# Second attention of a fused two-layer block: the scalings of a batch move into the route of the batch ahead, ranks move behind the values, the output bias becomes one product, and the powers on GpSimd change place

## The reference

```
x = x + 0.5 * _L0_ffn_ref(_layernorm(x), ...)
x = x + _L0_attn_ref(_layernorm(x), ...)
x = x + 0.5 * _L0_ffn_ref(_layernorm(x), ...)
x = x + 0.5 * _L1_ffn_ref(_layernorm(x), ...)
x = x + _L1_attn_ref(_layernorm(x), ...)          # the change is here
x = x + 0.5 * _L1_ffn_ref(_layernorm(x), ...)     # its route overlaps the line above

def _L1_attn_ref(x, Wq, bq, Wk, bk, Wv, bv, Wo, bo):
    q, k, v = x @ Wq + bq, x @ Wk + bk, x @ Wv + bv
    # 7 windows of 128 rows, each 64 rows on from the last
    scores = einsum('bwqd,bwkd->bwqk', q[win], k[win]) / sqrt(8)
    out_w = einsum('bwqk,bwkd->bwqd', softmax(scores), v[win])
    out = (sum of the windows over each row) / counts
    return out @ Wo + bo

def _L1_ffn_ref(x, router_w, router_bias, ...):
    scores = softmax(x @ router_w.T + router_bias)          # 32 experts
    topk_scores, topk_idx = top_k(scores, 4)
    ...                                                     # the 4 experts' outputs, weighted, and 4 shared experts
```

## Time and profile before

| | us |
|---|---|
| median of 3 runs | 938.57 (936.98 to 939.16) |
| the profiled execution | 937.39 |
| its span | 936.2 |
| PE busy | 765.0 (82%) |
| DVE busy | 545.2 (58%) |
| ACT busy | 427.6 (46%) |
| POOL busy | 495.7 (53%) |

### The profile page before, as it was taken

The page is one execution under the profiler, slowest core; times in us unless marked ns, Lnnn a source line. Parts: engine busy times, 40 slices in busy tenths (PEclk is TensorE's granted clock), DMA queues, the critical chain, the costliest instruction groups (busy, mean ns, idle before and its releaser), DMA issues.

```text
span 936.2 us, 18891 instructions
## 1 busy us (share of the span) xinstructions
PE 765.0 (82%) x6432; PEld 622.5 (66%) x6432; DVE 545.2 (58%) x1655; ACT 427.6 (46%) x1099; POOL 495.7 (53%) x488
## 2 busy tenths in 40 slices
PE   6889978999999998798997999727888997999600
PEld 5778746589877876677775888614566775888500
DVE  6875576668577668977773444305855563444305
ACT  3667545656055536465422666501433322666500
POOL 5655630026291026376672677775177751677773
PEclk9999989999799989999999999958988999999955
DMA  9999999800140050011114444215011112444216
GB/s 227 218 217 212 224 220 220 179 4 4 48 135 1 2 158 1 1 47 41 45 56 111 124 122 126 72 53 185 1 50 50 50 43 74 120 124 123 75 53 230
DMA packets 125757, 94.67 MB, mean 101 GB/s; under 512 B 10624, under 2 KB 116480, under 8 KB 125664
## 3 DMA queue, kind: packets, MB, share of 16 engines
q1 hardware_dynamic: 113472, 71.19, 32.9%
q0 software_dynamic: 10176, 21.65, 6.7%
q10 hardware_dynamic: 2016, 0.63, 0.3%
HBM read 34.05 MB, written 59.38 MB: 100 GB/s over the span
## 4 chain that ended last, share of the span: by engine, by line
PE 47%; DVE 22%; POOL 14%; issue 9%; ACT 5%; DMA 2%; SPq 0%; POOLq 0%; DVEq 0%; ACTq 0%
POOL expert_rows L677 9%; PE banks L1638 5%; PE banks L1110 3%; POOL sorted_rows L445 3%; PE banks L1685 3%; PE banks L1667 3%; PE banks L624 3%; PE banks L783 3%; PE banks L172 3%; PE banks L396 3%; PE banks L397 2%; PE banks L398 2%; DVE h L744 2%; PE banks L793 2%; ACT sg L691 2%
## 5 line engine op out<-in xcount | busy, mean ns | idle before, releaser
L677 POOL DMA_INDIRECT expert_rows<-y,goal x190 | 181.9, 957 | 96.5 <-issue 53.7
L445 POOL DMA_INDIRECT sorted_rows<-rows_x,row_of x128 | 128.3, 1003 | 76.5 <-DVE row_of L500 40.2
L990 ACT ACTIVATE ys<-banks,wtab 128x128 f32<-128x128 f32 x256 | 73.0, 369 | 66.7 <-PE banks L1110 56.7
L744 DVE TENSOR_TENSOR h<-sg,banks 128x512 f32<-128x512 f32 x48 | 33.0, 687 | 97.3 <-ACT sg L691 97.3
L396 PE MATMUL banks<-x_high,w_high 128*128 128x512 f32 x192 | 85.3, 444 | 0.6 <-POOL w_low L880 0.6
L1110 PE MATMUL banks<-w,hT 128*128 128x128 f32 x512 | 72.9, 287 | 14.0 <-DVE hT L1031 13.9
L1110 PEld LDWEIGHTS banks<-w,hT 128*128 128x128 f32 x512 | 66.4, 197 | 23.3 <-DVE hT L1031 20.8
L915 POOL TENSOR_TENSOR x<-ys,x 128x512 f32<-128x512 f32 x44 | 56.3, 1280 | 45.2 <-ACT ys L990 44.7
L398 PE MATMUL banks<-x_high,w_low 128*128 128x512 f32 x192 | 76.8, 400 | 0.0
L397 PE MATMUL banks<-x_low,w_high 128*128 128x512 f32 x192 | 76.6, 399 | 0.0
L172 PE MATMUL banks<-wqkv,ident 128*128 128x384 f32 x122 | 53.0, 592 | 26.2 <-DMA expert_rows<-y,goal 19.4
(11 more groups left out here) (300 smaller groups left out, 1884.4 us busy)
## 6 DMA issues: line engine op xcount, KB each, us to landing
sorted_rows<-zeros SPq DMA_DIRECT2D x32, 1120.0 KB, 17.1
tile<-sorted_rows SPq DMA_DIRECT2D x192, 70.0 KB
routed_low<-in_ffn_w SPq DMA_DIRECT2D x8, 512.0 KB, 3.8
w<-in_ffn_w SPq DMA_DIRECT2D x20, 192.0 KB, 3.9
expert_rows<-y,goal POOLq DMA_INDIRECT x190, 2.2
routed_down<-in_ffn_w SPq DMA_DIRECT2D x8, 256.0 KB, 5.2
sorted_rows<-rows_x,row_of POOLq DMA_INDIRECT x128
xnT<-expert_rows SPq DMA_DIRECT2D x2, 1024.0 KB, 5.7
```

Source lines behind the costliest of these rows:

```text
L445: POOL.indirect_dma_start(sorted_rows, bass.IndirectOffsetOnAxis(self.row_of[:, g, i:i + 1], 0), rows_x[:, 4 * g + i % 4, :], None).then_i ...
L677: POOL.indirect_dma_start(expert_rows, bass.IndirectOffsetOnAxis(goal[:, 4 * q + i:4 * q + i + 1], 0), y[q % 6][:, i * P:(i + 1) * P], Non ...
L990: last = SCL.mul(ys[s % 2][:, j * P:(j + 1) * P], bank[4 + s % 2][:, j * P:(j + 1) * P], wtab[:, t, e:e + 1])
```

## The change

- The loop over batches on DVE: `scale(b, 0)` and `scale(b, 1)` stand behind the pieces "scores" and "top" of the route of group b-1, no longer behind all of its pieces.
- `vector_low(b - 1)` stands behind `residual(b)` and the piece "variance".
- PE: `tensor_rank(b - 1)` stands behind `values(b, 1)`, no longer ahead of `turned(b, 0)`; of the two `keep_busy(3, ...)` around it, one with 2 products is left.
- `output`: one 128x512 product of ones with the bias row, broadcast over the four blocks, comes ahead of the wait for `oT`; the four 128x128 products with `Wo` add to it.
- POOL: the next group's power comes behind the 3rd transfer of group 0, the 1st of group 1 and the 1st of group 2, no longer behind the 8th.

```diff
-                for b, transfers in enumerate((8, 8, 8, 0)):
+                for b, transfers in enumerate((3, 1, 1, 0)):
                     srt.pool_dispatch(b, transfers)
...
                         maximum(b, 0)
                         maximum(b, 1)
-                        for piece in Sorted.VECTOR[2:]:
+                        for piece in ("scores", "top"):
                             routed_piece(b - 1, piece)
                         scale(b, 0)
                         scale(b, 1)
-                        srt.vector_low(b - 1)
+                        for piece in ("hot", "counted", "weights", "rows"):
+                            routed_piece(b - 1, piece)
                     residual(b)
                     routed_piece(b, "variance")
+                    if b:
+                        srt.vector_low(b - 1)
...
                 def output(b):
+                    PE.wait_ge(*(norm.ready(b + 1) if b + 1 < B else srt.norm.ready(b - 1)))
+                    PE.matmul(bank[6][:, :], ones[:, :], bo_row[:, :].unsqueeze(1).broadcast_to([P, TB, D]), start=True, stop=False,
+                              skip_group_check=True)
                     PE.wait_ge(*oT_ready(b + 1))
-                    PE.wait_ge(*(norm.ready(b + 1) if b + 1 < B else srt.norm.ready(b - 1)))
                     for j in range(TB):
-                        po = bank[6][:, j * P:(j + 1) * P]
-                        PE.matmul(po, oT[b % 2][:, j * P:(j + 1) * P], wo1[:, :], start=True, stop=False)
-                        last = PE.matmul(po, ones[:, :], bo_row[:, :], start=False, stop=True)
+                        last = PE.matmul(bank[6][:, j * P:(j + 1) * P], oT[b % 2][:, j * P:(j + 1) * P], wo1[:, :], start=False,
+                                         stop=j == TB - 1, skip_group_check=True)
...
-                        keep_busy(3, bank[5 - b % 2])
-                        srt.tensor_rank(b - 1)
-                        keep_busy(3, bank[5 - b % 2])
+                        keep_busy(2, bank[5 - b % 2])
                     turned(b, 0)
                     turned(b, 1)
                     values(b, 0)
                     values(b, 1)
+                    if b:
+                        srt.tensor_rank(b - 1)
                     if b < LAST:
                         project_q(b + 1)
                     output(b)
```

## The result

The changed kernel took 926.1 us (median of 4 runs, 923.33 to 929.95) beside 938.87 us for the kernel before (4 runs, 936.98 to 940.64): ratio 0.9877, 95% interval 0.9836 to 0.9918. Forecast were 924.9 us and a range of 923.0 to 932.0. The four executions stand in two pairs: 923.33 and 923.53 us at a mean granted clock of 0.925, 928.67 and 929.95 at 0.919 and 0.917. The profile is of the first pair: 923.53 us (span 922.3) against 937.39 (936.2, 0.928), 13.9 us less, where the sum gave 13.7. The second pair left no profile.

The account below looks back on a forecast made before the run. Two paths bounded the routed experts' start, PE's loop with shared steps and POOL's 64 transfers; with PE's loop shorter, POOL bounds. The tiles' turn moves from 783.21 to 769.5, 13.7 us sooner: 938.57 becomes 924.9 us, range 923.0 to 932.0.

Parts of the forecast that it names:

- the sum: POOL's transfers and powers, data, issue and landing added up: tiles' turn at 769.5 against 783.21, 13.7 us sooner.
- Scalings within the route: DVE's scalings start behind "top", so PE's `turned` comes 5.12 us sooner in batch 1; group 0's rows wait 1.49 us longer.
- Ranks behind the values: On PE, the 0.91 us rank moves behind the values without a wait, putting 0.91 us ahead of q and output.
- Bias as one product: One 512-column product of 0.86 us on PE, ahead of oT: no PE time saved, 0.5 us gained in batch 0.
- Fillers: Four of six PE fillers per batch go; they stood in waits for DVE and cost nothing if the clock holds.
- `vector_low`: Its 0.68 us go into DVE's 2.17 us wait for the power; delays batch 3's first shared `hT` by 0.6 us.
- Powers: On POOL, group 1's power comes at 683.8 without POOL waiting; group 1's transposes at 686.2, 5.3 us sooner.
- POOL is the bound: From group 1's transposes POOL's transfers and powers set the pace; transposes of group 2 at 704.9, group 3 from 726.2.
- The landing: First tiles' data arrive 3.9 us after SP's issue, between 3.2 and 6.05, so the turn comes at 769.5.
- (a): PE's clock stays low from group 1's transposes to batch 2's output, POOL waits 6.2 us: 931.1 us; chance 0.14.
- (b): PE's clock low throughout, from group 0's transposes to the shared steps: 5.4 us slower, 944.0 us; chance 0.03.
- (c): Powers or rows late through an unseen wait; PE's loop 2 us shorter a batch, not 5: 934.5 us; chance 0.09.

Follow-up runs that it names:

- e4: Changed kernel with the ranks again ahead of the transposes of the scaled weights (`turned`): 939.86 us, ratio 0.9964 to the kernel before.
- c2: Changed kernel measured again without any edit, on a third chip: 932.38 us, ratio 0.9864 to the kernel before.
- e6: Changed kernel without the 2 filler products ahead of `turned`: 936.75 us, ratio 0.9915 to the kernel before.
- f1: Changed kernel with the powers again behind 8 transfers of each group: 952.03 us, ratio 1.0076 to the kernel before.
- f2: Kernel before with only the powers moved, behind transfers 3, 1 and 1: 940.46 us, ratio 0.9960 to the kernel before.
- c1: Changed kernel again without any edit, in a session with all times much longer: 1085.43 us, ratio 0.9936 to the kernel before.
- c3: Changed kernel again without any edit, in another session with all times much longer: 1072.98 us, ratio 0.9969 to the kernel before.
- e3: Changed kernel with 2 more filler products ahead of each routed group's transposes, in a slow session: 1088.20 us, ratio 0.9970 to the kernel before.
- e5: Changed kernel with the output bias again as four products behind oT's wait, in a slow session: 1080.20 us, ratio 1.0022 to the kernel before.
- g1: Changed kernel, 3 filler products ahead of `turned`, 2 more ahead of transposes in batches 2 and 3, slow session: 1075.23 us, ratio 0.9981 to the kernel before.

## Why the prediction was right

| step | predicted | measured |
|---|---|---|
| `turned`, batch 1 | 673.84 | 673.81 |
| output's end, batch 1 | 680.3 | 680.28 |
| POOL's first transfer | 679.8 | 679.80 |
| power, group 1 | 683.8 | 683.37 |
| transposes, groups 1, 2, 3 | 686.2, 704.9, 726.2 to 726.8 | 685.79, 704.55, 726.05 |
| powers, groups 2, 3 | 702.5, 723.8 | 702.14, 723.64 |
| POOL's end, data | 764.0, 765.4 | 764.07, 765.41 |
| issue, turn of tiles | 765.6, 769.5 | 765.63, 769.34 |

**Scalings within the route** held to 0.03 us, with the wait of 1.3 us. **Ranks behind the values** took 0.81 us, not 0.91, and nobody waited for them but DVE in batch 3 (0.26 us). `e4` shows that the place matters more than its expectation had it. No run moves the scalings alone; their 5.1 us are read from the rows. **Bias as one product**: 0.86 us as taken, 0.5 gained in batch 0. **Fillers** cost nothing in the profiled execution; that part of the step was too sure, since with the same program the clock fell in `c2` and took 1.5 us. **`vector_low`** stood in a wait. **Powers**: the first came 0.4 us early, because POOL's first transfer took 1.03 us and not the 1.44 of the earlier trace rows, and the powers of groups 2 and 3 were 0.4 and 0.2 early with it; by the end that was given back, since two transfers took 1.16 and 1.15 us and one 1.01 instead of 0.96. That POOL's end came out to 0.1 us is in this part luck: two sizes were off and cancelled. The variance of group 2 was called just in time, at 701.9 to 702.7; it was there at 700.65, 1.5 us ahead of its power. From transposes to `turned` the sum took 6.0 us "as in batch 1" and 0.6 for a low clock, but its own batch 1 gives 5.49 (668.85 to 674.34), and it was 5.48 again. The power did not wait, so the time is the same. **POOL is the bound**: no gap over 0.31 us. The filler ended at 768.49 and PE then stood 0.85 us for tiles, so the data path decides. The landing took 3.71 us from the issue, where 3.9 was taken between 3.2 and 6.05.

The median of 926.1 is 1.2 us above the forecast, because two of the four executions took some 5 us more than the other two. The sum has no term for that. It had said that 0.2% could be told from no change; the interval came out at 0.4% to either side.

Of the rivals, (a) had the clock low from group 1's transposes to output. They did bring a low clock (`keep_busy` at 688.58 took 2.77 us for its 2 products, 1.46 in batch 1), but `turned` at 691.27 ran at full speed again (1.22 us), 0.91 over the batch. The slow filler only used up what had been 1.31 us of wait in batch 1, so the fall cost nothing. The Trainium skill (TensorE: Matmul & The Clock Gate, Part 4: PE-mode transpose) says that transposes do not count as busy for the clock as products do. By that rule rival (a)'s 931.1 should have come; the trace gave the forecast's time, and the falls in `c2` and `e6` came at transposes with 1.31 and 2.60 us of idle ahead of them, so no run here tells the rule from the idle. Rival (b), low clock throughout, is what `e4` has in part (0.91, 0.85, 0.80 by batch): still 0.4% faster than before. Rival (c) didn't come either in the changed kernel; `e4` is nearest to it, with `turned` meeting a wait, and lost 7.5 us beside 934.5 less 924.9 = 9.6.

What the prediction didn't say is how little its two main steps are worth apart: the powers alone gained 4.7 us by the medians, the order alone lost 7.1. It added their effects on one timeline, which was right for both together.

## What to carry to other kernels

Where a queue does two jobs, look for a ring: the producer's work waits for something that stands in the queue behind the consumer's items. Add up the pieces of the ring from the trace; if they make the period exactly, a faster producer alone is worth nothing, and a change of order that delays the items makes it slower. Then lay the changed timeline out to the queue's end and ask which engine has no gap left. Ask it again for each part of the change alone: here the turn waited for POOL's path in the changed kernel, `c2` and `e6`, and for PE's in the kernel before, `f1`, `f2` and `e4`.

## What the runs showed of the hardware

- PE's granted clock fell or held for the same instructions with the same idle of 1.31 us: 13.0 or 11.47 us to the rows, in 4 and 3 profiles.
- Of the powers on POOL for the routed groups, all 14 that began within 0.2 us of the start of DVE's `vector_low` (L507) took 1.41 us (`c1`, `c3`, `e3` to `e6`, `g1`); the others took 1.04 or 1.05, also behind waits of 5.32 and 2.85 us in `f2`, where `vector_low` is done by then. In the changed kernel it ends 0.08 us before the first power.
- The first indirect transfer after a wait took 1.44 us in the kernel before, where `scale` (L1863) ran on DVE as it began (678.62 to 679.31), and 1.03 in the changed one, where DVE was waiting. The 24 transfers of this route that took over 1.12 us, in all 14 profiles together, all lie beside L507, L1863 or L471, two-input operations on DVE; many others that do, too, took 0.96. No run was made to test this.
- On the same chip the kernel before took 945.2 us in one session and 1076.99 in a later one. The changed kernel's profile of the later one (`c3`) has waits of 7.5 and 8.9 us after the PE instructions waited for had ended.
